# Moving the weight preparation behind the first chunks, the first top layer's bias as a 512-column row, and one PSUM bank for all of it, in a DLRM tower on one core

## The reference

```python
e = jnp.stack([tbl_f[ids[:, f]] for f in range(26)], axis=1)      # 512 x 26 x 64
x = layer_norm(dense_t @ Wd.T, gd, bd)                            # 512 x 128
y = layer_norm(jnp.einsum('bnd,ed->bne', e, Ws), gs, bs)
y = layer_norm(jnp.einsum('bne,pn->bep', y, Wsi), gsi, bsi)       # 26 fields -> 32 slots
T = jnp.concatenate([x[:, None, :], jnp.swapaxes(y, 1, 2)], axis=1)
Z = jnp.einsum('bnd,bmd->bnm', T, T)                              # 33 x 33 pairs
out = layer_norm(Z[:, TRIL_I, TRIL_J] @ Wl.T, gl, bl)             # 528 -> 512, 384 kept
h = jnp.concatenate([out * mask, r_dense_t], axis=1)
h = jnp.maximum(h @ W_top1 + b_top1, 0.0)                         # 768 -> 512
h = jnp.maximum(h @ W_top2 + b_top2, 0.0)                         # 512 -> 256
y = h @ W_top3                                                    # 256 -> 1
```

## Time and profile before

| | |
|---|---|
| median of 3 runs | 248.82 us (247.56 to 250.93) |
| profiled execution, first to last instruction | 247.7 us |
| TensorE matmul busy | 173.4 us (70%) |
| VectorE busy | 131.7 us (53%) |
| ScalarE busy | 110.8 us (45%) |
| GpSimd busy | 109.4 us (44%), 105.3 of it in the 104 gathers |
| mean granted TensorE clock | 0.780 of full speed |

### The profile page before, as it was taken

How to read it: one execution, slowest core, us unless ns; L and a number is a source line. 1 busy time by engine, 2 the same in 40 slices (tenths; PEclk the granted TensorE clock), 3 DMA queues, 4 the chain that set the end, 5 groups by cost and what they waited for, 6 DMA issues and landing times.

```text
span 247.7 us, 4597 instructions
## 1 busy us (share of the span) xinstructions
PE 173.4 (70%) x1791; PEld 130.3 (53%) x1791; DVE 131.7 (53%) x273; ACT 110.8 (45%) x294; POOL 109.4 (44%) x110
## 2 busy tenths in 40 slices
PE   0569704982896772949939539689577686975996
PEld 0319703251453631836719329458365675664995
DVE  6365301527557184298672903738828473778412
ACT  2021032151647272573323673973206998356524
POOL 3787773775728274377460840865710000330000
PEclk9995555597599595685976857959959978897699
DMA  6604453111101011011010110111100000000000
GB/s 163 196 17 128 111 154 95 30 27 21 23 11 22 14 24 22 5 24 27 16 29 0 24 21 4 23 21 21 21 11 0 0 0 0 3 0 5 0 3 0
DMA packets 5728, 8.14 MB, mean 33 GB/s; under 512 B 2357, under 2 KB 3279, under 8 KB 5712
## 3 DMA queue, kind: packets, MB, share of 16 engines
q0 software_dynamic: 3328, 3.41, 7.7%
q1 hardware_dynamic: 1664, 3.65, 4.8%
q10 hardware_dynamic: 720, 0.85, 1.2%
HBM read 7.91 MB, written 0.00 MB: 32 GB/s over the span
## 4 chain that ended last, share of the span: by engine, by line
PE 43%; issue 22%; ACT 11%; another core or an unknown queue 10%; DVE 8%; POOL 3%; DMA 2%; ACTq 0%; DVEq 0%
PE ps_z L1011 8%; PE ps_y L991 6%; PE ps_tail L1026 6%; PE ps_gq L970 5%; PE ps_tail L1049 4%; PE ps_ut L981 4%; POOL G L285 3%; ACT zb L400 3%; DVE var L709 2%; PE ps_tail L954 2%; PE ps_gq L964 2%; DMA G<-in_table_dram,idx 2%; PE ps_y L1026 2%; ACT sq L381 2%
## 5 line engine op out<-in xcount | busy, mean ns | idle before, releaser
L285 POOL DMA_INDIRECT G<-in_table_dram,idx x104 | 105.3, 1013 | 74.6 <-PE ps_ut L981 37.4
L1011 PE MATMUL ps_z<-V 128*32 128x34 f32 x1024 | 23.2, 216 | 29.2 <-issue 27.4
L1011 PEld LDWEIGHTS ps_z<-V 128*32 128x32 f32 x1024 | 16.8, 125 | 38.2 <-issue 36.1
L970 PE MATMUL ps_gq<-gram,gt 128*128 128x128 f32 x104 | 20.3, 349 | 23.3 <-ACT gt L367 14.7
L681 DVE TENSOR_TENSOR qg<-ps_gq,G 128x384 f32<-128x384 f32 (+1 forms) x16 | 9.4, 589 | 43.3 <-PE ps_gq L970 28.7
L970 PEld LDWEIGHTS ps_gq<-gram,gt 128*128 128x128 f32 x104 | 17.3, 248 | 25.1 <-ACT gt L367 15.2
L400 ACT COPY zb<-zt 32x64 f32 (+1 forms) x96 | 28.5, 297 | 4.4 <-DVE zt L757 3.1
L709 DVE TENSOR_REDUCE var<-sq 128x32 f32<-128x1024 f32 x16 | 19.4, 1214 | 13.3 <-ACT sq L381 12.7
L981 PE MATMUL ps_ut<-S,G 128*128 128x192 f32 (+4 forms) x128 | 24.6, 343 | 2.2 <-issue 2.2
L991 PE MATMUL ps_y<-ut,wcg 64*128 64x512 f32 x64 | 23.0, 796 | 3.0 <-ACT ut L376 2.8
L981 PEld LDWEIGHTS ps_ut<-S,G 128*128 128x128 f32 x128 | 23.1, 225 | 2.6 <-issue 2.4
(11 more groups left out here) (138 smaller groups left out, 241.9 us busy)
## 6 DMA issues: line engine op xcount, KB each, us to landing
G<-in_table_dram,idx POOLq DMA_INDIRECT x104
w1z<-in_w_z_dram SPq DMA_DIRECT2D x1, 768.0 KB
wl<-in_wl_blocks_dram SPq DMA_DIRECT2D x1, 768.0 KB
dns<-in_dense_t_dram ACTq DMA_DIRECT2D x1, 512.0 KB, 6.3
w1d<-in_w_d_dram SPq DMA_DIRECT2D x1, 512.0 KB
wl<-in_wl_blocks_dram SPq DMA_DIRECT2D x1, 512.0 KB
w2s<-in_w_dram SPq DMA_DIRECT2D x1, 512.0 KB, 3.5
wrow<-in_wsi_rows_dram SPq DMA_DIRECT2D x1, 208.0 KB
```

The source lines that it names most:

```text
L285: pool.indirect_dma_start(G[:, j, g, :], None, table, bass.IndirectOffsetOnAxis(ap=idx[:, k:k + 1], axis=0)).then_inc(gathered[c], 16)
L970: mm = pe.matmul(ps_gq[:, n * P:(n + 1) * P], gt[:, n * P:(n + 1) * P], gram[:, :], start=True, stop=True)
L1011: mm = pe.matmul(ps_z[32 * qb:32 * qb + 32, bb // 8, col:col + SLOTS], V[:, b, 0:NPROJ], V[:, b, :], start=True, stop=True)
```

## The change

- `b_top1` is no longer a column block of `small` but a row `b1_row` of 512 numbers with a small load of its own, on SyncE's queue behind `w1z`. `b1e` becomes a row of 512 numbers.
- `prepare_b1`: three products with one stationary column and 512 moving columns instead of twelve with one moving column; VectorE adds the row.
- `prepare_dense(oc)`: a third product (one row by 512 columns) adds the bias in PSUM, and ScalarE copies without a bias. All four use `ps_tail`, so each waits for the copy before it. `pair_products` no longer waits for two dense copies but only for `x_sd_ready`.
- The order changes on three engines. TensorE: `prepare_b1` from behind `gram_rows(0, 0)` to behind `embed(0, 0)`; `prepare_xsum` and `prepare_dense(0)` from behind `embed(0, 0)` to behind `embed(0, 1)`; `prepare_dense(1)` to behind `embed(0, 2)`, the place of `prepare_last_block`, which goes behind `embed(0, 3)`. ScalarE: `prepare_w1` behind `square2(0, 0)`; `prepare_xsum`, the dense copies, `prepare_means(1)` and `prepare_last_block` later; the gains split as (0, 1) and (2, 3, 4), both in the first half of group 1. VectorE: `prepare_x` and `prepare_b1` behind `variance1` and `scale_rows` of chunk 1; `prepare_last_block` behind `variance2(0, 2)`; `prepare_shift` later.

```diff
+            sp.dma_start(b1e[:, :], b1_row).then_inc(ld_w1z, 16)
...
 ScalarE:
-                act.wait_ge(b1_ready, 1)
                 act.wait_ge(dense_ps, oc + 1)
-                act.activation(h1_dense[:, oc, :], dense_bank(oc), ACT.Identity, bias=b1e[:, oc:oc + 1]).then_inc(dense_ready, 1)
+                act.copy(h1_dense[:, oc, :], ps_tail[:, :]).then_inc(dense_ready, 1)
...
                 deviation2(gp - 1, 3)
-                prepare_gains((3, 4))
                 deviation1(gp, 1)
+                prepare_dense(2)
+                prepare_gains((0, 1))
                 z_copy(gp - 1, 0, (0, 1))
...
-                prepare_dense(2)
                 deviation1(gp, 2)
                 deviation2(gp, 0)
+                prepare_gains((2, 3, 4))
                 z_copy(gp - 1, 1, (0, 1))
...
             deviation1(0, 0)
-            prepare_w1()
             gt_copy(0, 1)
             ut_copy(0, 0)
             deviation1(0, 1)
             square2(0, 0)
+            prepare_w1()
             gt_copy(0, 2)
             ut_copy(0, 1)
-            prepare_xsum()
-            prepare_dense(0)
             deviation2(0, 0)
             deviation1(0, 2)
+            prepare_xsum()
             prepare_means(0)
-            prepare_dense(1)
+            prepare_dense(0)
...
 VectorE:
             prepare_x_root(1)
+            variance1(0, 1)
+            scale_rows(0, 1)
             prepare_x()
             prepare_b1()
-            variance1(0, 1)
-            scale_rows(0, 1)
             x_slots(0, 0)
...
 TensorE:
-                pe.wait_ge(ld_w1z, 16)
+                pe.wait_ge(ld_w1z, 32)
                 pe.wait_ge(ld_sm, 16)
-                for oc in range(OC1):
-                    for k in range(LLIVE):
-                        mm = pe.matmul(ps_tail[:, oc:oc + 1], w1z[:, k, oc * P:(oc + 1) * P],
-                                       sm[:, C_BL + k:C_BL + k + 1], start=(k == 0), stop=(k == LLIVE - 1))
+                for k in range(LLIVE):
+                    mm = pe.matmul(ps_tail[0:1, :], sm[:, C_BL + k:C_BL + k + 1], w1z[:, k, :],
+                                   start=(k == 0), stop=(k == LLIVE - 1))
                 mm.then_inc(b1_ps, 1)
...
                 for k in range(2):
-                    mm = pe.matmul(dense_bank(oc), w1d[:, k, oc * P:(oc + 1) * P], dns[:, k, :],
-                                   start=(k == 0), stop=(k == 1))
-                mm.then_inc(dense_ps, 1)
+                    pe.matmul(ps_tail[:, :], w1d[:, k, oc * P:(oc + 1) * P], dns[:, k, :], start=(k == 0), stop=False)
+                pe.matmul(ps_tail[:, :], b1e[:, oc * P:(oc + 1) * P], zx[ROW_ONE:ROW_ONE + 1, :],
+                          start=False, stop=True).then_inc(dense_ps, 1)
...
                     # pair_products, first
-                    pe.wait_ge(dense_ready, 2)
+                    pe.wait_ge(x_sd_ready, 1)
...
             gram_rows(0, 0)
-            prepare_b1()
             transpose_rows(0, 1)
...
             embed(0, 0, first=True)
-            prepare_xsum()
-            prepare_dense(0)
+            prepare_b1()
...
             embed(0, 1)
-            prepare_dense(1)
+            prepare_xsum()
+            prepare_dense(0)
```

More of the change, by code:

```diff
@@ L64 @@
 ROW_ONE, ROW_X, ROW_XV, ROW_S = 0, 32, 64, 96
-C_GD, C_BD, C_GL, C_BL, C_B1 = 0, 1, 2, 2 + LLIVE, 2 + 2 * LLIVE
-C_B2 = C_B1 + OC1
+C_GD, C_BD, C_GL, C_BL = 0, 1, 2, 2 + LLIVE
+C_B2 = 2 + 2 * LLIVE
 C_W3 = C_B2 + OC2
@@ L213, in dlrm_tower @@
         yo_ps, yo_ready, stored = sem("yo_ps"), sem("yo_ready"), sem("stored")
-        def dense_bank(oc):
-            return ps_z[:, oc, :] if oc < 2 else ps_tail[:, :]
         def z_bank():
@@ L492, in slots23 @@
                 if first:
-                    prepare_means(1)
+                    prepare_dense(1)
                 square2(gp, 2)
@@ L498, in slots23 @@
                 deviation2(gp, 2)
+                deviation1(gp + 1, 0)
                 if first:
+                    prepare_means(1)
                     prepare_last_block()
-                deviation1(gp + 1, 0)
-                if not first:
+                else:
                     square2(gp, 3)
                     z_evacuate(gp, 0)
-                else:
-                    prepare_gains((0, 1, 2))
             def last_slots(gp):
@@ L629, in prepare_b1 @@
             def prepare_b1():
-                dve.wait_ge(ld_sm, 16)
                 dve.wait_ge(b1_ps, 1)
-                dve.tensor_tensor(b1e[:, :], ps_tail[:, 0:OC1], sm[:, C_B1:C_B1 + OC1], ALU.add).then_inc(b1_ready, 1)
+                dve.tensor_tensor(b1e[:, :], ps_tail[0:1, :], b1e[:, :], ALU.add).then_inc(b1_ready, 1)
             def prepare_x_root(h):
@@ L824, in slots23 @@
                 if first:
-                    prepare_shift()
+                    prepare_last_block()
                 variance1(gp + 1, 0)
                 normalise2(gp, 2)
+                y_evacuate(gp, 3)
+                scale_rows(gp + 1, 0)
+                variance2(gp, 3)
                 if first:
-                    scale_rows(gp + 1, 0)
-                y_evacuate(gp, 3)
-                if not first:
-                    scale_rows(gp + 1, 0)
-                variance2(gp, 3)
+                    prepare_shift()
             def root2(gp, c):
@@ L929, in prepare_dense @@
                 if oc == 0:
-                    pe.wait_ge(x_sd_ready, 1)
-                if oc == 2:
+                    pe.wait_ge(xsum_ready, 1)
+                elif oc == 2:
                     pe.wait_ge(last_ready, 1)
-                if oc == 3:
-                    pe.wait_ge(dense_ready, 3)
+                else:
+                    pe.wait_ge(dense_ready, oc)
                 for k in range(2):
-                    mm = pe.matmul(dense_bank(oc), w1d[:, k, oc * P:(oc + 1) * P], dns[:, k, :],
-                                   start=(k == 0), stop=(k == 1))
-                mm.then_inc(dense_ps, 1)
+                    pe.matmul(ps_tail[:, :], w1d[:, k, oc * P:(oc + 1) * P], dns[:, k, :], start=(k == 0), stop=False)
+                pe.matmul(ps_tail[:, :], b1e[:, oc * P:(oc + 1) * P], zx[ROW_ONE:ROW_ONE + 1, :],
+                          start=False, stop=True).then_inc(dense_ps, 1)
             def prepare_xsum():
@@ L1136, in slots23 @@
                 else:
-                    prepare_last_block()
+                    prepare_dense(1)
                 transpose_rows(gp + 1, 0)
@@ L1142, in slots23 @@
                 embed(gp, 3)
+                if first:
+                    prepare_last_block()
                 pair_products(gp, 0, first)
@@ L1244, in lay_out @@
     o["small"] = sm
+    o["b1_row"] = a["b_top1"].reshape(1, H1)
     slot = np.arange(NPROJ)
```

10 lines of the change are left out of this document (4 added, 6 removed).

## The result

| | before | changed |
|---|---|---|
| median | 249.88 us of 4 (247.56 to 250.99) | 250.34 us of 4 (248.45 to 252.57) |
| ratio, changed to before | | 1.0151, 95% interval 1.0077 to 1.0225 |
| profiled execution, first to last instruction | 247.7 us | 250.7 us |
| mean granted TensorE clock | 0.780 | 0.816 |

The change costs 1.5%: the interval lies wholly above 1, and it reaches across 2%, so that the kernel is slower, by how much is open. The forecast was 244.2 beside 248.8, 2% faster. The profiled execution is the longest of the four, so up to 2 us of a row's lateness at the end may be its own.

A forecast was written before the change was run, and what follows sets the result against it. It took TensorE (43% of the chain) and its signals, late while POOL gathers without pause, as the bound. Earlier pair products −6.0, gains +1.4: span 247.7 − 4.6 = 243.1, plus 1.1 gives 244.2 us; own range 240.5 to 247.

The forecast's parts named there:

- the count again: TensorE parts since the first gather: bias products reach 54, the next two signals cross 48 to 56; gram_rows(0, 2) at 50.8.
- rival A: The new bias signal is late as well: gram_rows(0, 2) at 55.8, pair products end at 82.2, 248.8 us; chance 0.22.
- The rule behind the count: During unbroken gathers, TensorE's parts pass to about 50, then they and their signals crawl until 0.8 to 3.3 us after POOL's pause.
- POOL's run: With project_fields' signal in time, POOL doesn't pause at 38.56 but gathers on until about 48.9.
- the second late place: Before the change, gram_rows(0, 2) and prepare_dense(1) were seen late, the latter 7.2 us; no late signal expected between 50 and 62.
- The wait for x: embed(0, 0) on TensorE waits for VectorE's x, made behind chunk 1's steps: start at 34.9, 7.6 us ahead of before.
- From gram_rows(0, 2) on: TensorE from 50.8 through embed, xsum, dense(0) and projection: signal at 59.2; pair products end at 77.2, gain taken as 6.0.
- rival B: As rival A with TensorE's low clock: pair products end near 86.5, 254.1 us; chance 0.13.
- The last block: Moved behind embed(0, 3) on TensorE: start near 70, end near 75; POOL's run decides when pair products finish.
- The third products, the load and the bank: Third product 1.0 us per dense share; load free unless landing passes 37 us; bank's 0.69 copies hidden except for xsum.
- Gains, +1.4 us: ScalarE, group 1: gains (2, 3, 4) take 2.2 us ahead of z_copy, where 0.85 was idle: 1.4 us lost.
- Rival C: Crawl unrelated to gathers: gram_rows(0, 2) at 48.0, pair products start 71.5, take 8 us; 247.1 us; chance 0.15.

The follow-up runs named there:

- e9: The changed kernel with the bias products, x, VectorE's bias addition and ScalarE's scaling in their old places, under the crawl: 247.58 us, ratio 1.0089 to before.
- e6: The kernel before, unaltered, run again in a set without the crawl: 195.68 us (one run).
- e8: The changed kernel with VectorE's prepare_x ahead of variance1(0, 1) again, without the crawl: 205.30 us, 1.053 of before by the medians.
- e11: The kernel before with the new bias form and ScalarE's gains in their new places, under the crawl: 245.68 us, ratio 1.0029 to before.
- e15: e9's kernel run again in a set without the crawl: 199.04 us, ratio 1.0214 to before.
- e7: The kernel before with only the new bias form (row, three products, third product in each dense share), without the crawl: 194.53 us, ratio 0.9996 to before.
- e17: The changed kernel with dense products 0 and 1 in ps_z's two banks again, without the crawl: 210.22 us, ratio 1.0661 to before.
- e18: e15's kernel with dense products 0 and 1 in ps_z's banks again and two more waits on POOL, without the crawl: 200.00 us, ratio 1.0256 to before.
- e5: The changed kernel, unaltered, run again in a set without the crawl: 211.57 us, 1.085 of before by the medians.

## Why the prediction was wrong

*What failed: the step "the count again", at the bias signal.* It took the six bias products, with parts 49 to 54, to be seen at 42.3 and only the two signals behind them to be caught. The bias signal was seen at 52.50, that is rival A, to which I had given 0.22. I had written down the evidence for A myself, a late signal at part 48, and set against it that 55 parts had once passed in 15.5 us. So gram_rows(0, 2), forecast at 50.8, stood at 57.81, 7.0 us later. The runs show that the comparison of counts was empty: the first late signal of the changed kernel is at part 42, in e9 at part 48 already 8 us late (35.70), and in e6 1279 parts pass.

*The rule behind the count.* I had read that late signals come free 0.8 to 3.3 us after POOL pauses. The rows before spoke against it: the bias signal came free at 33.3, while POOL gathered on to 38.56. In all six traces with a crawl the first late signal comes free in the middle of a run of gathers, between 31.8 and 35.8, ahead of a pause at 38.56 (before) or at 47.8 to 48.3 (the five others). And of the slow stretches' starts I had given 56, 56 and 56 parts; the windows at 74.02 and 135.96 of the same trace had 52 and 64.

*The bias products' signal and what stands behind it.* A gave gram_rows(0, 2) at 55.8; it is 57.81, since the signal came 2.3 us later than POOL's old pause had suggested. The chain behind it, 5.5 us in A, took 5.3 (52.50 to 57.81).

*POOL's run.* Forecast to about 48.9, measured 48.16: right. ut_copy(0, 0) in time, and the second late place gone: right.

*The wait for x.* Forecast 34.9, measured 38.55, because gram_rows(0, 1) was itself caught. Without a crawl 33.07, so the estimate of the work was sound. But e8 shows what I missed by asking only when embed(0, 0) stands: there the same wait costs 6.3 us.

*From gram_rows(0, 2) on.* Forecast 19.2 us to the start of the last block (near 70), measured 20.1. That it came out is luck in part: in e9 gram_rows(0, 2) stands at 50.23, where the forecast had it, and the last block starts at 77.91 all the same, 27.7 us later, most of it at the low clock. My sum took the high clock there, and only rival B had the low one. So two things stood in the way of the forecast, the late bias signal and the clock, and moving the first away alone gained at most 2 us at the end of the first pair products (84.84 against 86.87). In the changed kernel the pair products ended at 86.87, 4.5 us after their start, against 77.2: by the rows, 7.0 of these 9.7 us stand at gram_rows(0, 2) already, and most of the rest is a crawl of the pair products, which I had taken to end with an earlier run of gathers.

*The last block.* I let its new place pass without a price, because the gathers would decide. Under the crawl it, the late dense shares and the one bank together make the 1.9 us between e9 and e11. Without it, it is the greater part of the 5.6 us of e15.

*The third products, the load and the bank.* Costed near nothing: e7 agrees (0.9996, without a crawl); for the bank no price can be told from nothing (e17, e18).

*Gains, +1.4 us.* e11 gives +0.7 us with an interval from −0.3 to +1.7 (ratio times 246.19): it doesn't tell 0 from 1.4. Between the first pair products and the end the changed kernel lost nothing (3.3 us late, then 3.0).

*From span to time.* The 1.1 us were too few: all runs that are listed with their spans show 1.8 to 1.95 (252.57 and 250.7, for one). With them the same sum gives 244.9, still below before.

*Rival B* didn't occur in the changed kernel: dense(0) ran at 1.95 us for four parts, the high clock's 1.98, and the last block at 4.53 for ten. In e9 it did. *Rival C* didn't occur as I had put it, since the late signals stayed with the new order. Its cause, that the crawl has nothing to do with gathers, isn't decided. For the gathers speaks that in all traces with a crawl the stretched pair products end 1 to 4 us after a run of gathers has ended. But that order is partly forced, since POOL's next gathers wait for products that TensorE does behind the pair products. The first late signals came free amid gathers, gathers alone are not enough, as e6 shows, and no kernel in which POOL pauses more often met a crawl. The rule of the Trainium skill ("SBUF — State Buffer", "Who interferes with whom"), that a DMA never contends with a compute engine, is neither borne out nor refuted by these runs. What causes the crawl stays open.

The larger error lies ahead of all steps: I built a count on one execution's late signals without asking whether they belong to the program. Looking back, the plain order of the steps pointed the other way, since the wait for x, the bias chain on three engines and two steps taken out of gather waits all add to the path; e5 to e8 and e15 measured that only without a crawl.

## What to carry to other kernels

Here a step of 4.56 us ahead of a wait for a transfer cost nothing, and behind that wait it stood on the path at its full length: before moving a step, look at the idle time behind its old place. When a signal is late for no visible reason, look at the same kernel on another chip before making the lateness a rule, and price the change both with and without it. Mends that gave 7 to 12 us under one condition gave nothing that could be told from noise under the other, so measure a change of order in both. And when a stage is moved forward, look at the granted clock behind it: e9's lead of 7.6 us was gone 19 us later.

## What the runs showed of the hardware

The same program took 194 to 195 us in four sets and 246 to 250 in two (medians), with gathers of the same length (1017 ns in e6, 1013 in before). What differs is TensorE: with the crawl its 1024 pair product parts show 29.2 us of idle time before them in the kernel before, without it 5.3. The groups by line of this same kernel, without the crawl (e6) and then with it:

```profile
L1011 PE MATMUL ps_z<-V 128*32 128x34 f32 x1024 | 14.5, 205 | 5.3 <-issue 2.1 <-DVE zt L757 1.8 <-DVE V L715 0.7
```

```profile
L1011 PE MATMUL ps_z<-V 128*32 128x34 f32 x1024 | 23.2, 216 | 29.2 <-issue 27.4 <-DVE zt L757 1.8
```

The stretches go in steps of about 0.7 and 1.4 us for one or two parts (83.17, 84.61, 85.36 above), and beside gathers a batch of pair products takes up to 10.7 us in the kernel before, against 1.3 without gathers and 1.9 to 2.1 beside gathers in e6. A low clock doesn't stretch them: from 82.38 to 85.36 the changed kernel's granted clock is 1.00. The mean granted clock is lower with the crawl (0.780 against 0.930), which may follow from the idle time. What sets the condition, the chip or something else that changed between the sets, wasn't found.
